# Weighted sums in blocks of one step, side work shared over 64 slots, and the first relus on ScalarE, in an attention and spiking feed-forward layer

## What is computed

```python
xn = _layernorm(x)
q = einsum('bnhd,hed->bnhe', xn.reshape(B, N, 16, 16), Wq)
attn = softmax(einsum('bnhe,bmhe->bhnm', q, q) / NORM)
s = einsum('bhnm,bmhe->bnhe', attn, q).reshape(B, N, D) @ Wp.T + bp
h = square(relu(einsum('bsd,fd->bsf', xn, W_fc)))     # 256 -> 1024
y = einsum('bsf,df->bsd', h, W_proj)                  # 1024 -> 256
# five steps: mem = 0.9 mem + y - (mem > 1); count (mem > 1)
g = silu(count / 5)
out = x + s * g
```

## Time and profile before

| | us |
|---|---|
| median of 3 runs (2578.52 to 2580.41) | 2579.01 |
| the profiled execution | 2580.22 |
| its span, first to last instruction | 2578.3 |
| busy: TensorE / ScalarE / VectorE / GpSimd | 2419.0 / 1983.1 / 1567.1 / 737.4 |
| exponentials, 2048 | 1941.9 |
| sums (records of L624), 8192 | 986.6 |

### The profile page before, as it was taken

One profiled execution on the slowest core, in us unless ns is written; L12 is line 12 of the kernel. 1 busy time (PEld: TensorE's weight loads), 2 busy tenths in 40 slices (PEclk: granted clock), 3 DMA queues, 4 the chain that ended last, 5 costly groups with the idle time before them and its releaser, 6 DMA issues.

```text
span 2578.3 us, 63759 instructions
## 1 busy us (share of the span) xinstructions
PE 2419.0 (94%) x23484; PEld 920.8 (36%) x23484; DVE 1567.1 (61%) x2581; ACT 1983.1 (77%) x2121; POOL 737.4 (29%) x681
## 2 busy tenths in 40 slices
PE   4999999999999999999999999999999999999997
PEld 2333333333333333333333333333333333333333
DVE  6456555766556675555765556665556755557664
ACT  2778778787777878778787787877778787787775
POOL 5123222333222332222332223332223332223420
PEclk7999999999999999999999999999999999999998
DMA  3011030210302102030110302102021120301200
GB/s 123 26 43 58 18 100 18 59 54 13 94 18 74 44 26 76 18 100 19 43 59 18 100 18 63 55 14 89 18 78 40 31 72 18 100 18 46 73 18 27
DMA packets 61487, 127.36 MB, mean 49 GB/s; under 512 B 15873, under 2 KB 17154, under 8 KB 58754
## 3 DMA queue, kind: packets, MB, share of 16 engines
q1 hardware_dynamic: 61186, 123.25, 15.5%
HBM read 89.11 MB, written 34.08 MB: 48 GB/s over the span
## 4 chain that ended last, share of the span: by engine, by line
PE 71%; ACT 14%; DVE 8%; issue 4%; SPq 1%; ACTq 0%; DMA 0%; DVEq 0%; POOL 0%; POOLq 0%
PE acc L624 34%; PE scores L650 18%; ACT e L804 14%; PE aux L541 8%; PE aux L550 7%; PE aux L532 2%; DVE cnt L931 2%; PE aux L598 1%; DVE r L913 1%; PE aux L556 1%; DVE h_t L919 1%; DVE acc_t L944 1%; SPq L447 1%; DVE q_hi L855 1%; DVE res L974 1%
## 5 line engine op out<-in xcount | busy, mean ns | idle before, releaser
L804 ACT ACTIVATE e<-scores 128x1024 f32<-128x1024 f32 x2048 | 1941.9, 1028 | 550.7 <-PE scores L650 550.5
L624 PE MATMUL acc<-e,v_ones 128*32 128x512 f32 x8192 | 986.6, 599 | 4.5 <-DVE acc_t L944 3.4
L650 PE MATMUL scores<-query_stack,key_stack 49*128 49x512 f16 x4096 | 712.6, 384 | 86.8 <-ACT e L804 59.4
L1176 POOL TENSOR_TENSOR r_squared<-r 128x512 f32<-128x512 f32 x256 | 266.5, 1041 | 996.2 <-DVE r L913 995.1
L541 PE MATMUL aux<-xn_t,w_fc 64*128 64x512 f16 x2976 | 454.7, 376 | 5.4 <-DVE xn_t L888 5.4
L550 PE MATMUL aux<-w_proj,h_t 64*128 64x256 f16 x6144 | 454.9, 270 | 1.3 <-DVE w_proj L901 1.3
L650 PEld LDWEIGHTS scores<-query_stack,key_stack 49*128 49x128 f16 x4096 | 158.9, 94 | 770.0 <-ACT e L804 726.7
L624 PEld LDWEIGHTS acc<-e,v_ones 128*32 128x32 f32 x8192 | 214.3, 109 | 464.6 <-issue 396.8
L550 PEld LDWEIGHTS aux<-w_proj,h_t 64*128 64x128 f16 x6144 | 334.8, 94 | 110.5 <-DVE w_proj L901 2.2
L1179 POOL TENSOR_TENSOR h_t<-r_squared,h_t 128x512 f16<-128x512 f32 x256 | 317.7, 1241 | 37.3 <-POOL r_squared L1176 1.7
L944 DVE STREAM_TRANSPOSE acc_t<-acc 128x512 f32<-128x512 f32 x128 | 91.2, 712 | 376.7 <-PE acc L624 376.7
(11 more groups left out here) (73 smaller groups left out, 980.3 us busy)
## 6 DMA issues: line engine op xcount, KB each, us to landing
key_stack<-q_scratch SPq DMA_DIRECT2D x384, 64.0 KB
query_stack<-q_scratch SPq DMA_DIRECT2D x384, 64.0 KB
x_tok<-x SPq DMA_DIRECT2D x16, 1024.0 KB, 5.0
x_out<-x SPq DMA_DIRECT2D x32, 512.0 KB, 3.7
out<-x_out SPq DMA_DIRECT2D x32, 512.0 KB, 2.7
q_scratch<-q_hi SPq DMA_DIRECT2D x32, 256.0 KB
q_scratch<-q_lo SPq DMA_DIRECT2D x32, 256.0 KB
query_stack<-c_scratch SPq DMA_DIRECT2D x128, 4.0 KB
```

Of the source, the lines that this page charges most:

```text
L624: ins = nc.tensor.matmul(acc[STRIP * n:STRIP * (n + 1), :], v_ones[:, j, G * g + n, :], e[:, tile, n % 2, :], start=j == 0, stop=j == TT - 1)
L650: return nc.tensor.matmul(bank, key_stack[base:base + 49, at, j * P:(j + 1) * P], query_stack[base:base + 49, at, half * HALF:(half + 1) * ...
L804: nc.scalar.activation(e[:, tile % NE, :, :], scores[tile % 2][:, :, :], ACT.Exp, scale=4.0 if exact else SCORE_SCALE).then_inc(s.exp_done, 1)
L1176: nc.gpsimd.tensor_tensor(r_squared[:, :], tile, tile, ALU.mult).then_inc(s.rsq_set, 1)
```

## The change

- Sums in blocks of one step: per step TensorE does `pv` of the step four back, a score tile, the side work of one slot, a score tile. `LAG` is now 4 steps, `BLOCKS` says for each step of a unit how many steps' sums it has (one each).
- Side work is shared over 64 slots, one a step, evenly (`SHARE` is 1 throughout); the stretches of an entry begin at steps 0, 15, 32 and 50, where they began at rounds 0, 9, 16 and 25 (steps 0, 18, 32, 50). First and last entry have their own.
- XT goes to the second stretch (slots 18 to 21, all on bank 0), Q to the first four of the third stretch's ninths, C to the sixth and seventh, on banks 1 and 2. Q's banks change. At the start the groups take the three banks in turn (`prep_bank`).
- The relus of the first eight FC groups go from VectorE to ScalarE (`relu_ahead`); `split_fold` and the split of w_proj move from behind the eight groups to among them.
- All tasks of VectorE and GpSimd have new times, on the scale of steps.

```diff
-ROUNDS = STEPS // ROUND
-LAG = 2
+LAG = 4
+BLOCKS = {i: 1 for i in range(8)}
+SHARE = [1] * 8
...
-BANK = {..., XT: [2, 0, 1, 2], Q: [0, 1, 2, 0], C: [1, 1]}
+BANK = {..., XT: [0, 0, 0, 0], Q: [2, 0, 1, 2], C: [1, 2]}
-PLAIN = [[(XT, 0)], [(XT, 1)], [(XT, 2)], [(XT, 3)], [(Q, 0)], [(Q, 1)], [(Q, 2)], [(Q, 3)], [(C, 0), (C, 1)]]
+PLAIN = {0: (Q, 0), 1: (Q, 1), 2: (Q, 2), 3: (Q, 3), 5: (C, 0), 6: (C, 1)}
...
+def prep_bank(n):
+    return n % 3
...
-    return (0, 0, 9, 21, 32) if first else (0, 9, 15, 24, 30) if last else (0, 9, 16, 25, 32)
+    return (0, 0, 22, 46, 64) if first else (0, 15, 30, 45, 60) if last else (0, 15, 32, 50, 64)
...
+        if n == 1:
+            whole = [(XT, k, (12 if first else 18) + k) for k in range(4)]
+        if n == 2:
+            at = [index for start, index in starts for half in range(9) if abs(start - 12 * half) < 1e-6]
+            whole = [(kind, k, at[half]) for half, (kind, k) in PLAIN.items()]
...
-                    for n in range(ROUNDS):
-                        for i in range(ROUND * (n - LAG), ROUND * (n - LAG) + ROUND):
-                            if i >= 0:
-                                pv(b, i)
...
-                        score_tile(b, 4 * n)
-                        score_tile(b, 4 * n + 1)
-                        for piece in rounds[n][0]:
-                            side(piece)
-                        score_tile(b, 4 * n + 2)
-                        for piece in rounds[n][1]:
-                            side(piece)
-                        score_tile(b, 4 * n + 3)
+                    for i in range(STEPS):
+                        for n in range(i - LAG, i - LAG + BLOCKS.get(i % TT, 0)):
+                            if n >= 0:
+                                pv(b, n)
+                            elif not first:
+                                pv(b - 1, STEPS + n)
+                        if i % TT in BLOCKS:
+                            score_tile(b, 2 * i)
...
+                        for piece in slots[i]:
+                            side(piece)
...
+                            score_tile(b, 2 * i + 1)
...
+                def relu_ahead(k):
+                    act.wait_ge(s.pe_done[FC], k + 1)
+                    wait(act, s.h_set, k - 1)
+                    nc.scalar.activation(r[:, k % 2, :], aux[BANK[FC][k]][:, :], ACT.Relu, scale=HS ** 0.5 / (XS * WS)).then_inc(s.relu_set, 1)
...
-                        tasks.append((-0.2, split_fold, ()))
-                        tasks.append((-0.1, split_lo, (w_proj16, proj_stage, proj_split)))
+                        tasks.append((-0.85, split_fold, ()))
+                        tasks.append((-0.65, split_lo, (w_proj16, proj_stage, proj_split)))
...
-                        at = unit * TT // ROUND + TT // ROUND + LAG - 1 + 0.42
+                        at = TT * unit + TT + LAG - 1 + 0.42
...
-                        stats_at, apply_at = (1.0, 4.6) if first else (5.7, 11.6)
+                        stats_at, apply_at = (2.3, 7.6) if first else (7.2, 12.6)
```

More of the change, by code:

```diff
@@ L119, in streams @@
              [(0, FC, k) for k in range(8)] + [(-1, PROJ, 2)]]
[L120 to L123, removed]
-def slot_starts(begin, end, lengths):
[L128 to L132, removed]
+    second = [[(0, Y, 0), (0, FC, 8), (0, Y, 1)], [(-1, PROJ, 3), (0, Y, 1), (0, Y, 0)]]
@@ L133, in slot_starts @@
     return starts
 def plan(first, last, exact):
-    rounds, ends = [[[], []] for _ in range(ROUNDS)], {}
+    slots, ends = [[] for _ in range(STEPS)], {}
     begins = stretches(first, last)
-    for n, pair in enumerate(streams(first, last)):
+    for n, (pair, lengths) in enumerate(streams(first, last)):
         if not pair[0]:
             continue
-        lengths = [60, 48] if n % 2 else [12] * 9
         starts = slot_starts(begins[n], begins[n + 1], lengths)
@@ L156, in plan @@
                     at += COLUMNS[kind]
[L157 to L159 removed]
+        opened = {pair[1][0]} if n != 1 or not first else set()
         for at, rows, group, i in sorted(pieces):
@@ L172, in plan @@
[L172 to L182, removed]
+                if i == PIECES[kind] - 1 and later:
+                    slots[slot].append(group + (None, 0, True, True))
+            else:
+                slots[slot].append(group + (rows, i, not later, later))
@@ new lines, in plan @@
+            if i == PIECES[kind] - 1 and later:
+                ends[group] = slot + 0.99
+        if last:
+            continue
+        whole = []
+        if n == 1:
[3 more added lines that the diff above has]
+            whole = [(kind, k, at[half]) for half, (kind, k) in PLAIN.items()]
+        for kind, k, slot in whole:
+            if not (exact and kind == C):
+                slots[slot].append((1, kind, k, None, 0, True, True))
+                ends[(1, kind, k)] = slot + 0.98
@@ L183, in plan @@
     if exact:
-        for slots in rounds:
-            for pieces in slots:
-                pieces.sort(key=lambda piece: piece[2] if piece[1] == Y else 0)
+        for pieces in slots:
+            pieces.sort(key=lambda piece: piece[2] if piece[1] == Y else 0)
     ahead = [(0, FC, k) for k in range(KF)] if first else []
@@ L189, in plan @@
         ends[group] = -1.0 + 0.1 * group[2]
-    return ahead, rounds, ends
+    return ahead, slots, ends
 def placed(first, last, at):
@@ L689, in body @@
                 def body(b, parity, first, last):
-                    ahead, rounds, _ = plan(first, last, exact)
+                    ahead, slots, _ = plan(first, last, exact)
                     if exact:
@@ L1077, in body @@
                         if kind == FC:
-                            tasks.append((at, relu, (b, k, bank)))
+                            tasks.append((at, relu, (b, k, bank, first and not exact and k < KF)))
                         if kind == Y and (last or k < 2):
```

119 lines of the change are left out of this document (71 added, 48 removed).

## The result

The changed kernel takes 2568.05 us (median of six runs, 2567.21 to 2571.09), the kernel before in the same comparison 2579.35 (2578.52 to 2581.21): ratio 0.9957, 95% interval 0.9945 to 0.997. The forecast was 2550: the kernel gained 11.3 us where 29 were forecast.

| us | forecast | measured |
|---|---|---|
| up to the loop's first step | -13.5 | 210.60 to 195.46: -15.1 |
| the 14 entries of the loop | -13 | 2187.60 to 2197.42: +9.8 |
| the last entry and what follows | -2.5 | 180.1 to 173.6: -6.5 |

What follows compares the result with a forecast made beforehand. TensorE was taken to pace the kernel, partly waiting for ScalarE's exponentials. Middle entries -13, start -13.5 and end -2.5 made -29 us: 2551 for the profile, 2550 for the median; own range 2538 to 2563, eight-in-ten range 2530 to 2577.

Steps and rivals of the forecast that it cites:

- group Q3: End of step 38: TensorE waits for bank 2, filled by FC10, behind VectorE's full order; 1.6 us an entry taken.
- rival (2): VectorE holds TensorE up more, long durations at group Q3, 4.5 us an entry: 2591 us; chance 0.12.
- -8.0 + 7.4: Middle entries: waits for ScalarE's exponentials go, 8.0 us an entry; more changes between sums and score tiles cost 7.4.
- The fixed part of a step: TensorE's time per step apart from pairs of side-work pieces: 1.59 of 2.23 us, plus 0.107 per pair.
- rival (4): Each added change of mode between sums and score tiles drains TensorE's whole array, 10.9 us for 7.4: 2602 us; chance 0.05.
- rival (3): Score tiles get no steadier, ScalarE still sets the middle entries' pace: 2561 us; chance 0.12.
- Bank waits: Loop: TensorE's waits for banks by C, transposes and fc pieces all go, 1.9 us per entry.
- I count no wait there: Handover of the sums through VectorE's transposition, eight times an entry: no wait counted in the new order.
- The reserve of 0.34 us: Handover of the sums: transposition over at 1.89 of a 2.23 us step, leaving 0.34 if VectorE stands ready.
- Start: First entry: tiles from about 46.4, then next entry's x holds step 12 until about 78.5; loop starts 13.5 us earlier.
- End: Last entry: no Q, same waits gained, smaller handover reserve; -2.5 us, between -6 and +1.
- rival 1: VectorE keeps up at group Q3, so no wait there, 1.6 us more gain in 14 entries: 2528 us; chance 0.15.

Runs made afterwards that it cites:

- the first try to free Q3: Changed kernel with only VectorE's order altered: five spike operations ahead of Q1, fourth unit's split sums behind Q3, two spike operations behind C1; 2543.3 us, ratio 0.9859.
- The old start: Changed kernel with the first eight relus back on VectorE and the splits of fold and w_proj behind all eight groups; 2574.04 us, ratio 0.9979.

## Why the prediction was right or wrong

**The step that failed is group Q3**: "So TensorE waits 1.4 us there", "I take 1.6". The mechanism was right: Q3 waits for FC10's h_t behind the split sums, Q2 and two spike operations, once an entry. The wait itself is 2.0 (and 0.23 of a late FC12 piece), within the bounds of 0 to 4.5; the operation that took longer beside GpSimd's work was not a spike operation, as I thought probable, but L991 of the split sums (by 0.84 us). What failed is the price: I took a wait to cost what it lasts, the bounds were bounds of its length alone, and the sum has no term for TensorE's clock. Steps 38 and 39 lose 2.3 us in four entries and 3.8 in ten, 3.4 on the mean, 2.3 of it the waiting and 1.1 the stretch at 1.2 GHz behind it. Taking away the wait gave back 3.46 an entry. The forecast named 3 us at Q3 as what would make it wrong, and rival (2) 3.7 as the point from which the kernel is slower than before; 3.4 lies between.

The middle entries, by the experiments (156.25 us before, 156.12 with blocks of two and no wait for Q3, 153.56 with blocks of one, 156.96 in the changed kernel):

| us an entry | forecast | measured |
|---|---|---|
| order, banks, sharing, without blocks and Q3 | -1.9 | -0.1 |
| blocks of one step | -8.0 + 7.4 = -0.6 | -2.6 |
| Q3 | +1.6 | +3.4 |
| sum | -0.9 | +0.7 |

The first two errors, +1.8 and -2.0, nearly cancel, which is luck; so Q3 makes the sum wrong.

- **Blocks.** The fixed part of a step is 2.19 - 6 x 0.107 = 1.55 us, not 1.59. In the last timeline with blocks of two, a round without its wait would be 1.86 + 0.44 + 0.69 + 0.22 + 0.69 + 0.32 = 4.22 (0.69 for six pairs in the first half too, as in the second), with blocks of one it is 4.38: the added changes of mode cost 0.16 a round, 5.1 us an entry and not 7.4, which rules out rival (4). No score tile waits for ScalarE any more in the loop, which rules out rival (3).
- **Bank waits.** C's, the transposes' and the one behind x's split are gone as forecast, but the order made a new one that costs 0.5 in step 8, which I had not looked for, and with blocks of two the transposes wait for xn_t (11.8 us in the loop); blocks of one hide that, so it counts in the second line.
- **Handovers of the sums.** "I count no wait there" held: 1.8 us for acc_t in the whole run, 1.58 of it the one forecast at step 12. The reserve of 0.34 us is real, though: the first try to free Q3 and blocks of one in the old order both ran past it.
- **Start.** The sums of step 12 were forecast at 78.5 and stand at 79.04, held by x of entry 1; loop at 197.1, measured 195.46. The way there was another in part: the first pieces of Y don't need all eight h_t, they start at 53.98, while GpSimd's chain ends at 57.42, behind 6.09 us of idle time that stay open. The old start shows that earlier tiles count for 0.4 us at the loop's first step; 12 of the 15 us come from blocks of one, which in the kernel before, too, bring that step from 210.60 to 200.69.
- **End.** -6.5 instead of -2.5, just outside the bounds of -6 to +1; the late handover of the earlier trace rows is gone. What else gained there was not tried.
- **VectorE keeping up** (rival 1, 2528) needed three other task times to come true: 2519.64. Rival (2), VectorE holding TensorE up more, came nearest to what the changed kernel does, but by the clock behind a wait of 2.0 us and not by a wait of 4.5 or late handovers.

## What to carry to other kernels

Price a wait of the engine that paces the kernel by what follows it as well as by its length: here 2 us of waiting cost 3.4, and a gain of 48 us hung on the place of six small operations (four spike operations, two transpositions) in another engine's order. Before a denser order is judged, list for each hand-over which tasks of the other engine stand ahead of it, and move those that nobody waits for. A block size and the order written for it are one change: each without the other was slower here than neither.

## What the runs showed of the hardware that was not expected

TensorE's clock in the loop follows its waits. Behind waits of 0.57 and 1.27 us it was 1.00. Behind waits of 1.98 us it fell in ten entries of 14 and stayed at 1.00 in four: in the changed kernel's profile in entries 1, 5, 9 and 13, in that of the old start, with the same wait, in 5, 8, 11 and 14. What decides between them is not shown. In the kernel with blocks of one and the old order it fell behind 25 of the 28 waits of 2.5 to 2.8 us (0.57 in the window shown), and behind 4.16 it was 0.54, with longer steps in all 14 entries. Each time in the windows read it was back at 1.00 a step or two later. The Trainium skill, "TensorE: Matmul & The Clock Gate", "HAM oscillation — how this bites in real kernels", says that waits for DMA between bursts of matmuls let the clock fall, so that each next burst starts slow. These rows agree that waits do it, here waits for another engine; the waits of its example are longer than the 1.98 us that were enough here.

VectorE's L991 in the split sums took 1.53 us at 1068.40, while GpSimd worked at h_t from 1068.23 to 1069.39, and 0.69 elsewhere in the same entry (1035.02), where GpSimd had nothing at work; so it was in all 14 entries. The Trainium skill, "SBUF — State Buffer", "SBUF: two separate sides", has the two engines share a pair of ports as an exclusive lock, for a VectorE operation with two inputs in SBUF against a GpSimd operation that reads SBUF. The row agrees: L991 reads two such inputs and ended 0.54 us behind GpSimd's operation.
